# A linear-recurrence layer on one Trainium2 core: the products k v go into the scan's own SBUF ring, with longer leads around it

## The reference, cut to what matters

```python
w = jnp.exp(-jnp.exp(time_decay + jnp.tanh(xw @ td_w1) @ td_w2)).reshape(b, l, h, s_)
r = (xr @ Wr.T).reshape(b, l, h, s_)
k = (xk @ Wk.T).reshape(b, l, h, s_)
v = (xv @ Wv.T).reshape(b, l, h, s_)
def step(s, rkvw):
    r_t, k_t, v_t, w_t = rkvw
    a = k_t[..., :, None] * v_t[..., None, :]
    out = jnp.einsum('bhi,bhij->bhj', r_t, u * a + s)
    s = a + w_t[..., :, None] * s
    return (s, out)
```

## Time and profile before

| | |
|---|---|
| median of 3 runs | 5423.05 us (5421.52 to 5426.53) |
| the profiled execution, its own time | 5408.33 us |
| its span | 5406.7 us |
| mean granted TensorE clock | 0.898 |
| TensorE, VectorE, ScalarE, GpSimd busy | 83%, 58%, 38%, 31% of the span |
| second layer's scans | from 1055.5 to 2158.5 us, 512 of them |

### The profile page before, as it was taken

The page is one execution under the profiler, slowest core; times in us unless marked ns, Lnnn a source line. Parts: engine busy times, 40 slices in busy tenths (PEclk is TensorE's granted clock), DMA queues, the critical chain, the costliest instruction groups (busy, mean ns, idle before and its releaser), DMA issues. The chain is left out here.

```text
span 5406.7 us, 77912 instructions
## 1 busy us (share of the span) xinstructions
PE 4510.6 (83%) x22864; PEld 3323.5 (61%) x22864; DVE 3115.6 (58%) x6291; ACT 2078.3 (38%) x3989; POOL 1669.2 (31%) x1127
## 2 busy tenths in 40 slices
PE   6999997678888887588888797997888977988886
PEld 3444443456666655377676586875676855877764
DVE  5555553356676667276673474754675744757642
ACT  2444444223333331244452353542444532544421
POOL 1223223244444444122224223223223233232240
PEclk8998998788888888799998898998899988999999
DMA  1000000200000000111112212112111122121123
GB/s 37 18 24 16 20 20 9 90 9 1 12 12 13 12 9 8 52 52 52 52 52 76 73 55 60 48 53 87 61 48 56 56 65 80 59 61 44 55 70 106
DMA packets 123228, 240.96 MB, mean 45 GB/s; under 512 B 16885, under 2 KB 34037, under 8 KB 121825
## 3 DMA queue, kind: packets, MB, share of 16 engines
q1 hardware_dynamic: 119520, 225.31, 13.2%
q0 software_dynamic: 3456, 12.58, 0.6%
HBM read 220.79 MB, written 16.78 MB: 44 GB/s over the span
## 5 line engine op out<-in xcount | busy, mean ns | idle before, releaser
L1744 POOL TENSOR_TENSOR c_wl<-c_wr,c_wh 128x512 fp32r<-128x512 f32 (+1 forms) x576 | 828.1, 1441 | 1925.4 <-ACT c_wh L1972 1681.2
L1790 PE MATMUL c_ps<-c_hh,c_wh 128*128 128x512 f32 x768 | 321.9, 419 | 145.0 <-POOL c_hl L1750 145.0
L2023 ACT ACTIVATE c_pr<-c_ps,c_nms 128x257 f32<-128x257 f32 x512 | 244.4, 478 | 484.3 <-DVE c_nms L2177 482.1
L572 ACT ACTIVATE a_ex<-a_ps 128x1024 f32<-128x1024 f32 x256 | 261.4, 1024 | 339.3 <-PE a_ps L408 339.1
L1790 PE MATMUL c_ps<-c_wh,c_cth 128*128 128x256 f32 x1024 | 300.2, 293 | 97.2 <-POOL c_wl L1744 97.2
L1389 POOL TENSOR_TENSOR b_sb<-b_sb,b_rt 128x1024 f32<-128x1024 f32 x128 | 291.0, 2274 | 272.4 <-DVE b_sb L1429 269.8
L1429 DVE TENSOR_TENSOR_SCAN b_sb<-b_wt,b_s,b_ps 128x256 f32<-128x256 f32 x512 | 350.6, 727 | 6.3 <-issue 3.5
L666 DVE TENSOR_REDUCE a_nm<-a_ps 128x2 f32<-128x1024 f32 x256 | 310.8, 1218 | 70.2 <-PE a_ps L385 67.1
L1972 ACT ACTIVATE c_wh<-c_wr 128x512 fp32r<-128x512 f32 (+1 forms) x448 | 302.1, 683 | 66.2 <-DMA c_wr<-in_wv 49.4
L1790 PE MATMUL c_ps<-c_gh,c_wh 128*128 128x512 f32 x768 | 311.3, 405 | 13.1 <-ACT c_g L2072 10.0
L1791 PE MATMUL c_ps<-c_hl,c_wh 128*128 128x512 f32 x768 | 319.7, 416 | 0.0
(11 more groups left out here) (314 smaller groups left out, 11233.6 us busy)
## 6 DMA issues: line engine op xcount, KB each, us to landing
c_wr<-in_downs SPq DMA_DIRECT2D x192, 256.0 KB, 2.7
c_wr<-in_wv SPq DMA_DIRECT2D x64, 512.0 KB, 4.3
c_wr<-in_wq SPq DMA_DIRECT2D x128, 256.0 KB, 2.8
c_wr<-in_wk SPq DMA_DIRECT2D x128, 256.0 KB, 3.2
c_wr<-in_fc SPq DMA_DIRECT2D x64, 256.0 KB, 2.8
b_w<-in_w SPq DMA_DIRECT2D x8, 1024.0 KB, 12.7
a_x<-in_x SPq DMA_DIRECT2D x8, 512.0 KB, 3.9
a_ctx<-in_ctx SPq DMA_DIRECT2D x8, 512.0 KB, 4.3
```

Source lines behind the costliest of these rows:

```text
L572: act.activation(EX[:, n % 4, :, :], ps[:, BT + 2 * (n % 2):BT + 2 * (n % 2) + 2, :], ACT.Exp).then_inc(ex_ready, 1)
L1744: pool.tensor_tensor(piece(WL, slot), piece(WR, slot), piece(WH, slot), ALU.subtract).then_inc(piece_cut[slot], 1)
L1790: pe.matmul(out, sh, mh, start=start, stop=False, skip_group_check=True)
L2023: act.activation(PR[:, i, 0:L + 1], ps[:, BS + 1 - i % 2, 0:L + 1], ACT.Exp, bias=NMS[:, i:i + 1], scale=float(K2) ** -0.5, accum_out=RS[: ...
```

## The change

The products are written to the ring in place of PSUM, and each scan reads and writes its ring columns in place. The ring has four quads. The spread is two quads ahead, also across the border of two batches, and needs only the multiply of two quads before, since that frees the banks. The gather is two quads behind. The multiply waits until its ring slot is free. The post stage's pieces move by up to four steps. To make room in SBUF for the fourth slot, the small tensors T1, RS and TW share one tensor, BB and TW2 go into an unused part of W2, and two loads at the layer's start go with them.

```diff
+        RING, AHEAD_Q, BEHIND_Q = 4, 2, 2
-        SB = sb("sb", [P, 3, 4, L + 1])
+        SB = sb("sb", [P, RING, 4, L + 1])
+        T1, RS, TW = TT[0:DM, :], TT[DM:DM + NH1, :], TT[DD:P, :]
+        BBR, TW2R = W2[DM:DM + NH1, 1, :], W2[DD:P, 1, :]
-        AT_GM, AT_GV, AT_BB, AT_WO, AT_MEAN, AT_VAR, AT_FK, AT_FR, AT_FV = 4, 10, 14, 22, 29, 33, 44, 51, 59
+        AT_GM, AT_GV, AT_BB, AT_WO, AT_MEAN, AT_VAR, AT_FK, AT_FR, AT_FV = 8, 13, 17, 25, 31, 35, 46, 53, 60
...
# spread
                 if quad >= 2:
-                    pe.wait_ge(s_ready, quad - 1 + AHEAD)
+                    pe.wait_ge(a_ready, quad - 1 + AHEAD)
...
# the loop of TensorE
-                    if scan is not None and n == 0:
-                        spread(scan, 0)
-                    if scan is not None and r == 0 and q + 1 < QUADS:
-                        spread(scan, q + 1)
+                    if b == 0 and n == 0:
+                        for first in range(AHEAD_Q):
+                            spread(0, first)
+                    if scan is not None and r == 0:
+                        ahead, quad = divmod(q + AHEAD_Q, QUADS)
+                        if scan + ahead < B:
+                            spread(scan + ahead, quad)
                     if r == 2:
-                        if scan is not None and q > 0:
-                            gather(scan, q - 1)
-                        if post is not None and q == 0:
-                            gather(post, QUADS - 1)
+                        if scan is not None and q >= BEHIND_Q:
+                            gather(scan, q - BEHIND_Q)
+                        if post is not None and q < BEHIND_Q:
+                            gather(post, QUADS + q - BEHIND_Q)
...
# states
-                if quad >= 3:
-                    act.wait_ge(y_used, quad - 2 + AHEAD)
+                if quad >= RING:
+                    act.wait_ge(y_used, quad - RING + 1 + AHEAD)
...
# multiply
-                dve.tensor_tensor(a, KT[:, b % 2, c, :].unsqueeze(1).broadcast_to([P, 4, L]), a, ALU.mult).then_inc(a_ready, 1)
+                if quad >= RING:
+                    dve.wait_ge(y_used, quad - RING + 1 + AHEAD)
+                dve.tensor_tensor(SB[:, quad % RING, :, 1:L + 1], KT[:, b % 2, c, :].unsqueeze(1).broadcast_to([P, 4, L]), a, ALU.mult).then_inc(a_ready, 1)
...
# scan_step
                 if r == 0:
                     dve.wait_ge(a_ready, quad + 1 + AHEAD)
-                    if quad >= 3:
-                        dve.wait_ge(y_used, quad - 2 + AHEAD)
-                mm = dve.tensor_tensor_scan(SB[:, quad % 3, r, 1:L + 1], WT[:, b % 2, c, :], half(spread_bank(quad, r), r), S0[:, b % 2, c, 4 * jq + r:4 * jq + r + 1],
+                mm = dve.tensor_tensor_scan(SB[:, quad % RING, r, 1:L + 1], WT[:, b % 2, c, :], SB[:, quad % RING, r, 1:L + 1], S0[:, b % 2, c, 4 * jq + r:4 * jq + r + 1],
                                             ALU.mult, ALU.add)
...
# the loop of VectorE
-                        if n == 0:
-                            multiply(scan, 0)
-                        if r == 3 and q + 1 < QUADS:
-                            multiply(scan, q + 1)
+                        if b == 0 and n == 0:
+                            multiply(0, 0)
+                        if r == 3:
+                            ahead, quad = divmod(q + 1, QUADS)
+                            if scan + ahead < B:
+                                multiply(scan + ahead, quad)
                         scan_step(scan, n)
-                    if post is not None and n == 3:
-                        take_sums(post, EC - 1)
-                    if scan is not None and n > 4 and n % 16 == 3:
-                        take_sums(scan, n // 16 - 1)
+                    if n % 16 == 4 * (BEHIND_Q - 1) + 3:
+                        c = n // 16 - 1
+                        if c < 0 and post is not None:
+                            take_sums(post, EC - 1)
+                        if c >= 0 and scan is not None:
+                            take_sums(scan, c)
```

More of the change, by code:

```diff
@@ L848, in layer1 @@
         T0 = sb("t0", [P, L])
-        T1 = sb("t1", [DM, L])
-        TW = sb("tw", [DD, L])
+        TT = sb("tt", [P, L])
         KT = sb("kt", [P, 2, EC, L])
@@ L990, in gather @@
                 for s in range(4):
-                    mm = pe.matmul(half(GATHER, c)[32 * s:32 * s + 32, :], SELG[:, jq, :], SB[:, quad % 3, s, 0:L], start=(jq == 0), stop=(jq == 3),
+                    mm = pe.matmul(half(GATHER, c)[32 * s:32 * s + 32, :], SELG[:, jq, :], SB[:, quad % RING, s, 0:L], start=(jq == 0), stop=(jq == 3),
                                    skip_group_check=True)
@@ L1039, in pre_stage @@
                     for o in range(2 * i, 2 * i + 2):
-                        mm = pe.matmul(half(PF, o), W2[strip, f // 4, o * P:(o + 1) * P], T0[strip, :] if f < 4 else T1[:, :], start=True, stop=True,
+                        mm = pe.matmul(half(PF, o), W2[strip, f // 4, o * P:(o + 1) * P], T0[strip, :] if f < 4 else T1, start=True, stop=True,
                                        skip_group_check=True)
@@ L1057, in pre_stage @@
                     for k in range(EC):
-                        mm = pe.matmul(half(PA, 0)[0:DD, :], TW1[:, k, :], XF[:, 0, k, :], start=(k == 0), stop=(k == EC - 1), skip_group_check=True)
+                        mm = pe.matmul(half(PA, 0)[DD:P, :], TW1[:, k, :], XF[:, 0, k, :], start=(k == 0), stop=(k == EC - 1), skip_group_check=True)
                     mm.then_inc(pa_ps, 1)
@@ L1064, in pre_stage @@
                     for o in range(2 * i, 2 * i + 2):
-                        mm = pe.matmul(half(PA, o), TW2[:, o * P:(o + 1) * P], TW[:, :], start=True, stop=True, skip_group_check=True)
+                        mm = pe.matmul(half(PA, o), TW2R[:, o * P:(o + 1) * P], TW, start=True, stop=True, skip_group_check=True)
                     mm.then_inc(pa_ps, 1)
@@ L1092, in post_stage @@
                     for c in range(EC):
-                        mm = pe.matmul(half(PB, 0)[0:NH1, :], BMC[:, c, :], SQB[:, c, :], start=(c == 0), stop=(c == EC - 1), skip_group_check=True)
+                        mm = pe.matmul(half(PB, 0)[DM:DM + NH1, :], BMC[:, c, :], SQB[:, c, :], start=(c == 0), stop=(c == EC - 1), skip_group_check=True)
                     mm.then_inc(gv_ps, 1)
@@ L1101, in post_stage @@
                     for c in range(2 * i, 2 * i + 2):
-                        mm = pe.matmul(half(PB, c), BB[:, c, :], RS[:, :], start=True, stop=True, skip_group_check=True)
+                        mm = pe.matmul(half(PB, c), BBR[:, c * P:(c + 1) * P], RS, start=True, stop=True, skip_group_check=True)
                     mm.then_inc(bb_ps, 1)
@@ L1388, in _ @@
                         pool.wait_ge(first_in, quad + 1 + AHEAD)
-                        pool.tensor_tensor(SB[:, quad % 3, :, 0:L], SB[:, quad % 3, :, 0:L],
+                        pool.tensor_tensor(SB[:, quad % RING, :, 0:L], SB[:, quad % RING, :, 0:L],
                                            RT[:, scan % 2, q // 4, :].unsqueeze(1).broadcast_to([P, 4, L]), ALU.mult).then_inc(y_ready, 1)
```

30 lines of the change are left out of this document (14 added, 16 removed).

## The result

The changed kernel takes 5430.4 us (median of 20 runs, 5422.2 to 5442.5) beside 5420.2 before (20 runs). The ratio is 1.0019, with an interval of 1.0012 to 1.0027: some 10 us slower. The number lies in the range of 5370 to 5530; the size of the forecast, +44 us, does not hold.

A forecast was written before the change was run, and what follows sets the result against it. No engine was full; TensorE came first, losing time to waits. Blocks +13.4 and relief -8.1 gave +5.3 us a batch, +37 over seven, +8 last batch, -1 start: +44, 5465 us; 8-in-10 range 5370 to 5530.

The forecast's parts named there:

- The port: Second layer's scans, now with two SBUF inputs, and GpSimd's SBUF work block each other: +13.4 us a batch on the path.
- rival 1: The scan does not block beside GpSimd, so the relief of 8.1 us a batch stays: 5360 us, chance 0.13.
- the difference L1375: Steps 39 to 44: GpSimd's subtraction falls between scans 41 and 42, ahead of the multiply spread 44 needs: 1.9 us.
- the gate behind the ring multiply: Step 39: GpSimd's ring multiply stands ahead of VectorE's L1471, which has two SBUF inputs: 2.2 us a batch.
- The 3.2 us at the mix of step 22: Steps 11 to 20: two blocks delay L1486, which ScalarE's scaling and then the mix wait for: 3.2 us.
- the 2.1 us of XK: Step 44: XK (L1501), now behind scan 44, meets the ring's multiply of quad 10: 2.1 us on FK.
- The blocked time in all: GpSimd's old timeline laid over the 64 scans: 22.3 us a batch, 13.4 on the path, 8.9 in VectorE's idle time.
- The leash and the moved steps: Second layer without blocking: waits removed by longer spread lead and moved steps, less new waits, sum to -8.1 us a batch.
- The moved steps' own waits: New waits a batch: +3.7 us at the second output product, +4.4 at the variance, +1.3 at G1's reading, 0.3 for gathering.
- The second: Rival: scans block but nearly all hides in VectorE's idle time, only 4.2 us a batch stays: 5398 us, chance 0.17.
- The third: Rival: VectorE becomes the bound, all 22.3 us of blocks a batch on the path: 5538 us, chance 0.12.
- The fourth: Rival: no measurable change, blocks and relief within 1.5 us of each other a batch: 5423 us, chance 0.13.

The follow-up runs named there:

- run 9: Changed kernel with all GpSimd arithmetic of the second layer replaced by memsets that read nothing, results left out: 5323.1 us, ratio 0.9824 to the kernel before.
- run 3: Changed kernel with products kept in PSUM and spread one quad ahead; moved steps, ring of four, later gather stay: 5396.4 us, ratio 0.9962 to the kernel before.
- run 5: Kernel before with only the nine moved steps of the post stage: 5408.4 us, ratio 0.9980 to the kernel before.
- run 4: Changed kernel with post-stage steps and gather lead as before; products in the SBUF ring, spread two ahead: 5425.6 us, ratio 1.0009 to the kernel before.

## Why the prediction was right or wrong

**The port: right in kind, and in size partly by luck.** Scans with two SBUF streams do stand still behind GpSimd, and GpSimd behind them (rival 1 falls: run 9's scans are at 734 ns, the changed kernel's at 1186, with the same instruction). The prediction's price was 13.4 us a batch and 13.7 for the last, 107 in all; run 9 and the changed kernel differ by 106. The size agrees better than its parts. The wait at the spread of 44 grows by 4.5 us, where the difference L1375 (1.9) and the gate behind the ring multiply (2.2) were put ahead of it: both stand there in the timeline above. That at 52 grows by 2.0 (2.3 put down), that at the variance by 2.7 (1.7 put down). The 3.2 us at the mix of step 22 are not there: that wait is 3.1 us with and without blocks. Nor do the 2.1 us of XK show, as FK's product waits no longer than in run 9 (0.2 to 0.7 us, against 1.0). In all TensorE's waits grow by 9 us a batch and not by 13.4. What makes up for it is TensorE's busy time, 114 us in run 9, 119 to 125 in the changed kernel: a clock term that the price did not have. A part follows the longer waits (the eight matmuls of the variance take 3.78 us behind 5.45 us idle, 1.99 behind 2.76); the 6 us between 119 and 125 are mostly the bonus.

**The blocked time in all: under-sized.** Laying the old timelines over each other gave 22.3 us a batch. The scans got 236 us longer over eight batches, 29.6 each. A likely reason, which no run isolates: in the old timeline VectorE waited 12.5 us a batch for spreads and some of GpSimd's work fell there; that time is gone. The prediction also gives VectorE's idle time as 39.8 us a batch; by the earlier trace rows it is 146.6 - 99.1 = 47.5. The path's 13.4 us do not hang on it.

**The leash and the moved steps: the step that failed.** The prediction puts them at -8.1 a batch, -63 in all with the last batch and the start; run 9 against the kernel before says -95. With the blocks right in total, this term alone turns the forecast +44 into some +10. Its list of waits came out well: 2.3 us at step 52 (2.25 measured in run 9), 3.1 at 44 (3.3), 2.0 at the second output product (2.0), less good for the variance (4.4, measured 2.8), and without the mix's 3.1, which it had booked as a block. A wait of 1.3 us at the spread of step 40 was not foreseen. TensorE's waits fell only from 22.5 to 18.8 us a batch between the kernel before and run 9, 3.7 where the terms of the prediction hold 6.2. The rest is the clock: busy time fell from 124 to 114, by 10 us where they hold 1.9. The prediction counted 1.7 or 1.8 us of slow matmuls at three places, two that go and one that comes, and left the slow stretch around the bonus as it was, without a reason. That is the failed step: this stretch did not stay as it was. In the kernel before all twelve groups of the bonus are slow, in run 9 two, in the changed kernel three. Whether it runs slow or not is worth 5.6 to 6.7 us a batch by itself, in the changed kernel (152.3 and 146.7) and in run 3 (146.8 and 140.1); the other 3 to 4 of the 10 us lie in other stretches. It is also why two of the changed kernel's four full batches are shorter than the 150 us that the prediction gave as the least. Why one batch finds the one level and the next the other, with waits that differ by 0.6 us at most, no run here settles. The moved steps alone do not decide it: two of the twelve are slow in run 5, nine in run 3 with the same steps, six in run 4 with the steps as before.

**The moved steps' own waits: mostly right one by one, wrong as a sum.** The prediction found new waits of +9.7 us a batch against gains of the moves of -6.2, by itself a loss. The moves alone gave a gain of 11 us in the whole (run 5).

**Rivals.** The second (all but 4.2 us a batch of the blocks hide) gave 5398; its bound, less than 8.1 us of blocks on the path, is not met, since the blocks are 13 a batch. The third (VectorE as the bound, 5538) falls by the time itself, and by the 17 to 25 us a batch in which VectorE is idle. The fourth, with a chance of 0.13, is what happened, by its own words too: blocks and relief within 1.5 us of each other a batch. 106 us of blocks stand against 95 of relief, 1.4 us a batch.

## What to carry to other kernels

When an operand moves from PSUM to SBUF, ask of every VectorE instruction that reads it whether it now has two SBUF inputs, and what GpSimd does meanwhile. Lay the two timelines over each other; a replacement that only writes on GpSimd measures the price in one run, with the same on the old kernel as control, if it is no shorter than what it replaces. Split a change that has a cost and a gain: here the part that needed no SBUF products (moved steps, later gather) was 21 us faster by itself, and the whole was 10 slower. Where a kernel's batches alternate between two lengths with the same waits, an estimate from waits alone is open by that difference.

## What the hardware showed that was not expected

A collision costs both engines. GpSimd's ring multiply went from 2274 to 2445 ns in the mean, while a scan beside GpSimd's work loses up to 2 us (the longest took 2.8 against 0.75 before). Moving such work to VectorE did not end it: 1465 ns in place of 1200 for the same multiply there.

The same instruction list with nearly the same waits on TensorE (23.1 and 22.5 us) ran a batch in 140.1 or 146.8 us, at a mean granted clock of 0.94 or 0.88. In the kernel before the slow stretch at the bonus stood in every batch; a change of leads and steps that does not touch the bonus took it out of most.
